# A selective scan on one NeuronCore: ScalarE writes each segment's summed first step into PSUM, contraction in four pieces

## The reference

```
def step(h, inputs):
    d_t, B_t, C_t, u_t = inputs
    dA = jnp.exp(d_t[:, :, None] * A)
    h = h * dA + (d_t * u_t)[:, :, None] * B_t[:, None, :]
    y_t = jnp.einsum('bdn,bn->bd', h, C_t)
    return (h, y_t)
...
_, ys = jax.lax.scan(step, h0, seq)
```

## Time and profile before

| | |
|---|---|
| time, median of 3 runs | 7032.84 us (7032.73 to 7033.88) |
| time of the profiled execution | 7032.57 us |
| its span in the profile | 7030.4 us |
| first scan starts, last scan starts | 1261.83 us, 6346.43 us |
| busy share of the span: PE, DVE, ACT, POOL | 87%, 83%, 42%, 24% |
| the same between 1400 and 5400 us: PE, DVE, ACT, POOL | 96%, 97%, 47%, 24% |

### The profile page before, as it was taken

One profiled execution on the slowest core, in us unless ns is written; L12 is line 12 of the kernel. 1 busy time (PEld: TensorE's weight loads), 2 busy tenths in 40 slices (PEclk: granted clock), 3 DMA queues, 4 the chain that ended last, 5 costly groups with the idle time before them and its releaser, 6 DMA issues. The chain is left out here.

```text
span 7030.4 us, 150993 instructions
## 1 busy us (share of the span) xinstructions
PE 6124.9 (87%) x46048; PEld 3347.2 (48%) x46048; DVE 5847.0 (83%) x5536; ACT 2985.0 (42%) x5218; POOL 1657.6 (24%) x4800
## 2 busy tenths in 40 slices
PE   2666553899999999999999999999999999997999
PEld 1222221455555555555555555555555555554666
DVE  7455544899999999999999999999999999994443
ACT  1544443344444444444444444444444444441111
POOL 4222223222222222222222222222222222220000
PEclk9777776999999999999999999999999999998999
DMA  4454556111111111111111111111111111113231
GB/s 136 153 168 167 178 193 202 36 32 35 33 36 33 33 35 32 35 33 36 33 33 35 32 36 33 34 34 33 35 32 36 33 34 34 32 31 119 98 116 60
DMA packets 1133035, 451.75 MB, mean 64 GB/s; under 512 B 762544, under 2 KB 1088816, under 8 KB 1132608
## 3 DMA queue, kind: packets, MB, share of 16 engines
q1 hardware_dynamic: 1088304, 421.73, 22.7%
q10 hardware_dynamic: 44688, 29.50, 1.3%
HBM read 229.72 MB, written 221.71 MB: 64 GB/s over the span
## 5 line engine op out<-in xcount | busy, mean ns | idle before, releaser
L883 DVE TENSOR_TENSOR_SCAN s_h<-s_decay,s_ubank 128x1024 f32<-128x1024 f32 x2048 | 4682.1, 2286 | 70.4
L849 ACT ACTIVATE s_decay<-s_abank 128x512 f32<-128x512 f32 x4096 | 2224.2, 595 | 2728.9 <-PE s_abank L806 2728.0
L816 PE MATMUL s_ubank<-s_x,s_w 128*128 128x128 bf16 x16384 | 2129.7, 309 | 195.2 <-DVE s_h L883 192.1
L789 PE MATMUL s_ybank<-s_h,s_window 128*16 128x256 f32 x16448 | 2088.8, 599 | 2.7 <-DVE s_h L883 2.7
L816 PEld LDWEIGHTS s_ubank<-s_x,s_w 128*128 128x128 bf16 x16384 | 1697.3, 129 | 340.0 <-DVE s_h L883 264.1
L918 POOL TENSOR_TENSOR s_carry<-s_decay,s_h 128x32 f32<-128x32 f32 x2016 | 588.9, 292 | 3594.4 <-ACT s_decay L849 3594.4
L806 PEld LDWEIGHTS s_abank<-s_x,s_a 128*128 128x128 bf16 x8192 | 647.1, 100 | 1638.9 <-ACT s_decay L849 1076.3
L806 PE MATMUL s_abank<-s_x,s_a 128*128 128x256 bf16 x8192 | 1270.6, 277 | 55.5 <-DMA s_w<-scratch_b_rows 55.5
L789 PEld LDWEIGHTS s_ybank<-s_h,s_window 128*16 128x16 f32 x16448 | 305.1, 97 | 534.3 <-issue 530.7
L921 POOL TENSOR_TENSOR s_decay<-s_none 128x32 f32<-128x32 f32 x2048 | 506.0, 247 | 160.3
L879 DVE TENSOR_TENSOR s_ubank<-s_ubank,s_carry 128x32 f32<-128x32 f32 x2048 | 368.9, 180 | 125.2 <-POOL s_decay L921 98.6
(11 more groups left out here) (116 smaller groups left out, 2852.9 us busy)
## 6 DMA issues: line engine op xcount, KB each, us to landing
scratch_u_rows<-p_u_turn SPq DMA_DIRECT2D x136, 512.0 KB, 6.9
scratch_delta_rows<-p_dparts SPq DMA_DIRECT2D x128, 512.0 KB, 5.7
s_x<-scratch_delta_rows SPq DMA_DIRECT2D x1024, 64.0 KB, 3.6
s_x<-scratch_u_rows SPq DMA_DIRECT2D x2048, 32.0 KB, 1.7
scratch_y<-s_y ACTq DMA_DIRECT2D x1032, 16.0 KB, 1.5
scratch_sz<-p_sz SPq DMA_DIRECT2D x16, 1024.0 KB, 8.7
scratch_u<-p_u SPq DMA_DIRECT2D x16, 1024.0 KB, 10.0
s_w<-scratch_b_rows SPq DMA_DIRECT2D x256, 64.0 KB, 2.4
```

The lines of the kernel that those rows point to most:

```text
L789: last = nc.tensor.matmul(y_bank[32 * ct:32 * ct + WIN, s, 0:PAIRS], window[:, s, t * WIN:(t + 1) * WIN], H[s][:, :, t], start=(tt == 0), ...
L816: last = nc.tensor.matmul(dst.rearrange("p q t -> p t q"), w2[:, g, 4 * s + e, :], x2[:, s, :, e, q:q + 16], start=True, stop=True)
L849: nc.scalar.activation(decay[:, k % RING, 16 * b:16 * b + 16, :], a_bank[:, b].rearrange("p j r t -> p (j r) t"), ACT.Exp).then_inc(exp_do ...
L883: nc.vector.tensor_tensor_scan(H[s][:, PT * k:PT * k + PT, :].rearrange("p q t -> p (q t)"), decay[:, k % RING].rearrange("p q t -> p (q t)"),
```

## The change

1. DVE's addition (line 879) and its semaphore `added` are gone. DVE waits for `seeded` and scans.
2. PE makes one more matmul a chunk, behind the exponent matmuls of tile 0: the input of the first step of all 256 pairs, 128x256 from operands of 16 bits, into a bank of its own (`s_firstbank`). To make room for it in PSUM, `s_ybank` has one place and not two, and the contraction waits until the copy of its predecessor is out.
3. ACT copies this bank to SBUF (`s_first`) in tile 0, and `take_y` moves from tile 1 to tile 0. In every tile, behind the two exponentials, ACT waits for the inputs of the tile and for POOL, and writes `s_seed` (128x32) over the first steps in `s_ubank`.
4. POOL gets an operation per tile between the other two: `s_seed` = `s_carry` + `s_first`.
5. The contraction stands behind tiles 1, 3, 5 and 7, two steps each. Before, it stood behind tiles 1 to 7, one step each and two behind tile 2.

```
@@ -59,9 +59,8 @@
-Y_TILE = 1
-CONTRACT = {1: (0,), 2: (1, 2), 3: (3,), 4: (4,), 5: (5,), 6: (6,), 7: (7,)}
+CONTRACT = {1: (0, 1), 3: (2, 3), 5: (4, 5), 7: (6, 7)}
@@ contract @@
-                    pe.wait_ge(y_read, f + 1)
+                    pe.wait_ge(y_read, f + 2)
@@ PE, chunk @@
                     if k == 0:
                         pe.wait_ge(u_loaded[s], it * 256 + (c // 2) * 128 + 128)
+                        pe.wait_ge(first_read, f + 1)
+                        nc.tensor.matmul(first_bank[:, 0:PAIRS], w2[:, g, 4 * s, :], x2[:, s, 0, 0, :],
+                                         start=True, stop=True).then_inc(first_ready, 1)
@@ ACT, chunk @@
-                    if k == Y_TILE:
+                    if k == 0:
+                        act.wait_ge(first_ready, f + 1)
+                        nc.scalar.activation(first[:, c % 2, :], first_bank[:, 0:PAIRS],
+                                             ACT.Identity).then_inc(first_read, 1)
                         take_y(f, c % 2)
+                    act.wait_ge(u_ready, n + 17)
+                    act.wait_ge(carried, n * 3 + 3)
+                    nc.scalar.activation(u_bank[:, k % 2, :, 0], seed[:, k % CPS, :], ACT.Identity).then_inc(seeded, 1)
                     if k == Y_STORE:
                         store_y(f, c % 2)
@@ DVE, chunk @@
-                    first = u_bank[:, k % 2, :, 0]
-                    dve.wait_ge(carried, n * 2 + 2)
-                    dve.wait_ge(u_ready, n + 17)
-                    nc.vector.tensor_tensor(first, first, carry[:, k % CPS, :], ALU.add).then_inc(added, 1)
                     if k == 0:
                         dve.wait_ge(y_ready, f + 1)
-                    dve.wait_ge(added, n + 1)
+                    dve.wait_ge(seeded, n + 1)
@@ POOL, chunk @@
                     nc.gpsimd.tensor_tensor(carry[:, k % CPS, :], decay[:, k % RING, :, 0], before,
                                             ALU.mult).then_inc(carried, 1)
-                    pool.wait_ge(carried, n * 2 + 1)
+                    if k == 0:
+                        pool.wait_ge(first_read, f + 2)
+                    pool.wait_ge(carried, n * 3 + 1)
+                    nc.gpsimd.tensor_tensor(seed[:, k % CPS, :], carry[:, k % CPS, :],
+                                            first[:, s, PT * k:PT * k + PT], ALU.add).then_inc(carried, 1)
                     nc.gpsimd.tensor_tensor(decay[:, k % RING, :, 0], none[:, :], none[:, :], ALU.mult).then_inc(carried, 1)
```

More of the change, by code:

```diff
@@ L707, in scan_stage @@
         carry = sb("s_carry", [P, CPS, PT])
+        first = sb("s_first", [P, 2, PAIRS])
+        seed = sb("s_seed", [P, CPS, PT])
         none = sb("s_none", [P, PT])
@@ L717, in scan_stage @@
         u_bank = ctx.enter_context(nc.psum_tensor("s_ubank", [P, 2, PT, T], F32))
-        y_bank = ctx.enter_context(nc.psum_tensor("s_ybank", [P, 2, 512], F32))
+        y_bank = ctx.enter_context(nc.psum_tensor("s_ybank", [P, 512], F32))
+        first_bank = ctx.enter_context(nc.psum_tensor("s_firstbank", [P, 512], F32))
         rows_loaded = [sem("rows_loaded0"), sem("rows_loaded1")]
@@ L728, in scan_stage @@
         carried = sem("carried")
-        added = sem("carry_added")
+        first_ready = sem("first_ready")
+        first_read = sem("first_read")
+        seeded = sem("seeded")
         scan_done = sem("scan_done")
@@ L788, in contract @@
                         t = ct * WSTEPS + tt
-                        last = nc.tensor.matmul(y_bank[32 * ct:32 * ct + WIN, s, 0:PAIRS],
+                        last = nc.tensor.matmul(y_bank[32 * ct:32 * ct + WIN, 0:PAIRS],
                                                 window[:, s, t * WIN:(t + 1) * WIN], H[s][:, :, t],
@@ L827, in _ @@
             act.sem_inc(exp_done, 2)
+            act.sem_inc(first_read, 1)
             for s in range(2):
@@ L834, in take_y @@
                 act.wait_ge(y_stored[s], (f - s) * 32 + 64)
-                nc.scalar.activation(yout[:, s, :], y_bank[:, s, 0:PAIRS], ACT.Identity).then_inc(y_read, 1)
+                nc.scalar.activation(yout[:, s, :], y_bank[:, 0:PAIRS], ACT.Identity).then_inc(y_read, 1)
             def store_y(f, s):
@@ L865, in _ @@
         def _(dve):
-            nc.vector.memset(y_bank[:, :, :], 0.0).then_inc(y_read, 1)
+            nc.vector.memset(y_bank[:, :], 0.0).then_inc(y_read, 1)
             nc.vector.memset(w2[:, :, :, :], 0.0).then_inc(cleared, 1)
@@ L901, in lay_window @@
                 pool.wait_ge(y_ready, f + 1)
-                pool.wait_ge(carried, n * 2 + 2)
+                pool.wait_ge(carried, n * 3 + 3)
                 for h in range(2):
```

## The result

The changed kernel takes **7580.14 us** (median of 4 runs, 7575.57 to 7583.31) against 7032.78 us for the kernel before (4 runs, 7031.98 to 7033.88): a ratio of 1.0778, 95% interval 1.0759 to 1.0796. It is 547 us slower; forecast were 538 us and 7570 us. The total agrees much better than its parts do: two sizes were wrong, and they cancel.

What follows compares the result with a forecast made beforehand. DVE and PE were taken to bound the kernel at 19.87 us a chunk; 8 x 2.38 + 1.83 + 1.00 + 0.10 = 21.97 us, 2.10 us more over 256 chunks, gave 7570 us, range 7330 to 7870 us.

Steps and rivals of the forecast that it cites:

- What bounds the kernel before: Scan stage: DVE (19.3 us a chunk alone) and PE (19.0 us) both full; ACT and POOL run ahead.
- The circle: ACT and POOL: the write waits for POOL, POOL for the tile's exponentials, the next tile's exponentials stand behind the write.
- The size of a turn: ACT and POOL, from write to write: 2.38 us a tile, above the 2.20 us of a scan.
- POOL's sum: POOL's new operation between product and zeroing: 0.37 us with a wait like the product's, lower bound 0.29 us.
- The hand-over to ACT: From the end of POOL's zeroing to ACT's write: 0.11 us, taken from POOL's hand-over to DVE.
- The path through the contraction: Behind tile 7, from tile 5's write to tile 0's: 8.14 us against 7.14 us, 1.00 us more a chunk.
- The stores: Four DMAs issued by ACT behind tile 3's write delay the next exponential: 1.83 us more, once a chunk.
- The start of ACT's loop: ACT's table load before tile 0's exponential, once in four chunks: 0.41 us, 0.10 us a chunk.
- The drain behind a table load: The skill's rule adds about 1.38 us to each ACT table load, some 88 us in all; the prediction left it out.
- a write as dear as a copy: Rival: ACT's write takes 0.39 us like the copy, 0.17 us more six times a chunk: 7830 us; chance 0.20.
- The gain: Rival: the turn hides behind PE and the scans, the stage can fall to PE's 18.8 us a chunk: 6760 us; chance 0.05.
- The clock: Rival: a less busy PE drops the scan stage's granted clock to 0.72: 8620 us; chance 0.03.

Runs made afterwards that it cites:

- reordering alone: Kernel before with exponents and exponentials of tile n+1 moved ahead of inputs, contraction and addition of tile n: 6884.74 us, ratio 0.9795.
- one of the kernels above: Changed kernel with next tile's exponents and exponentials moved ahead of inputs and write, ACT's loop over two chunks, stores issued by SP: 6769.65 us, ratio 0.9626.
- opening the circle with the same work: Changed kernel with next tile's exponents and exponentials moved ahead of inputs and write, ACT's loop over two chunks: 6834.97 us, ratio 0.9723.

## Why the prediction was right, and where only its total was

- **What bounds the kernel before**: right. Both engines full, one idle time of 0.5 us a chunk: reordering alone gave just the 145 us that follow from DVE's 19.3 us a chunk, and one of the kernels above runs at PE's floor of 18.8 us a chunk.
- **The circle**: right in kind. The write waits for POOL (1775 us in all), scans wait for the write (1043 us), and opening the circle with the same work gives back over 500 us (578 us with the table loads that leave the loop). One operation of 0.2 us in it costs 1.0 us a chunk.
- **The size of a turn**: 2.38 us forecast, 2.19 us measured. The term that was mis-sized is POOL's sum: 0.37 us, taken from an operation whose result the next one waits for; 0.21 us found, under the lower bound of 0.29 us, since the zeroing does not wait for the sum and starts before it ends. The hand-over to ACT was 0.03 us instead of 0.11 us, the start of the exponential 0.16 us instead of 0.11 us behind the write.
- **The path through the contraction**: right, and it binds at more places than I said. With the shorter turn it also sets tiles 6 and 2 (steps of 2.41 and 2.48 us, 0.2 to 0.3 us over the turn), where the text had it no later than the turns. The eight steps of a chunk make 21.1 us; forecast were 21.87 us.
- **The stores**: the step from tile 3 to 4 was 4.23 us (4.21 forecast). Their removal gives 1.0 us and not the 1.83 us of the sum, since the contraction of tile 3 runs beside them and binds next.
- **The start of ACT's loop**: the step of the sum that failed. I counted the start of a turn as the table load alone, 0.10 us a chunk; the long chunks cost 3.6 us each, 0.9 us a chunk. The missing term is the fetch of code, from the 100 instructions that the write and its waits add to a turn of ACT's loop (206 to 306). Nothing in the trace of before shows it, but the instruction queue with 22 packets and the growth of the loop could be read there and in the change. The two misses, 0.76 us too much a chunk in the steps and 0.8 us too little at the start of a turn, cancel: that the total came within 10 us is luck. The range would also have held the kernel without the long chunks (7413 us with two chunks a turn, 7330 being its lower end).
- **The drain behind a table load**: no such drain of 1.38 us in the changed kernel either (the exponential starts 0.01 us behind the load, at 1525.67 us), and ahead of the load it is 0.26 us with two chunks a turn. The Trainium skill ("ScalarE: Activation LUTs", "What ACT_TABLE_LOAD costs") gives its total for a switch to a different set of functions; whether these loads are one, no trace here shows.
- **The rivals**: a write as dear as a copy is out (0.20 us, 0.22 us forecast; the argument that the two lengths of the earlier trace rows lie on a line was empty, since any two do). The gain did not come through. The clock did not fall for the stage, it was granted at 0.98 on average in the window; but after most stalls of the long chunks it was, for some microseconds, at the lower level, which is worth some 40 us of the 547 us (below). The gain of the other side came with another order; a turn short enough to hide, 2.03 us by the prediction, was not tried.

## What to carry to other kernels

Before an operation is moved to an idle engine, ask what it will wait for there and what stands behind it in that engine's order: an engine that is 42% busy and ran ahead becomes the bound if it waits for the result of its own output. Write the work for the next tile ahead of such a wait; here this was worth over 500 us, and moving the operation was worth 50 us, or 115 us once the stores were off ACT too. Count the instructions of a loop's turn before and after an edit: a loop that no longer fits costs microseconds a turn, and it looks like an idle time behind nothing. Look for table loads inside a loop, too: with the first exponentials ahead of the loop they were gone from it.

## What the runs showed of the hardware that I had not expected

- The length of a loop's turn costs time: ACT loops of 306 and 412 instructions show about five packets more on the instruction queue per turn, and a gap ahead of the turn's first instruction, 2.5 to 2.9 us for 306 and 1.8 to 2.1 us for 412 (in the window from 1400 to 5400 us); 206 instructions show none.
- POOL starts an operation of 128x32 that has no wait 0.21 us behind the one before, which takes 0.25 us; with a wait for the one before, the step is 0.37 us.
- A table load stood at the head of each turn of ACT's loop (64 turns, 64 loads; with two chunks a turn 128) in the kernels that were not reordered; there the first exponentials came ahead of the loop, and the stage had one load in all.
- The clock after a stall. PE had stood idle for 2.42 us ahead of 1526.33 us; in a window right behind, the granted clock is 0.66, a mix of 1.2 and 2.4 GHz, and the eight input matmuls take 1.92 us and not 1.04 us; some microseconds later it is 1.00. It does not happen after every stall. Ahead of 1702.60 us PE had stood idle for 2.54 us, and the clock stayed at 1.00 (last two rows):

```profile
1526.00:1529.00 3.00, 2.58 (x16) 1.82 (x20) 1.07 (x1) 2.56 (x7) 0.75 (x3) 0.66 0.27 43
...
1532.00:1540.00 8.00, 6.48 (x59) 3.76 (x58) 4.99 (x4) 3.17 (x9) 2.75 (x11) 1.00 0.17 31
...
1700.00:1704.00 4.00, 1.36 (x12) 1.00 (x12) 0.19 (x1) 2.95 (x6) 0.75 (x3) 1.00 0.25 53
...
1703.32 1.04 PE L823 MATMUL s_ubank<-s_x,s_w 128*128 128x128 bf16 x8
```

The two kinds of turn separate the 3.6 us. The gap ahead of the table load is 2.7 us in both on average. In the 14 of 63 turns in which the clock stayed at 1.00 for 4 us behind the load, the long chunk takes 24.0 us on average, 2.9 us over an ordinary one; the gap and the table load do that alone. In the other 49 it takes 24.9 us, 0.84 us more with the lower clock. Over all turns the clock's part is 0.65 us (49 / 63 x 0.84), some 40 us of the total.
